# Neighbour sums of a graph network on one Trainium2 core: count strips in 4-byte form, source rows in two float32r parts instead of three bf16 parts

## What is computed

```python
def gin(x, src, dst, weights):                  # block 2
    for wa, ba, wb, bb in weights:              # 128->256->256, 256->256->256, 256->128->128
        h = x + segment_sum(x[src], dst)        # plain sums: every edge counts 1
        x = relu(relu(h @ wa + ba) @ wb + bb)
    return x
# block 4: h = segment_sum(norm_edge * (x @ W)[row], col), three times; norm from edge weights
x = layernorm(x + gat(x)); x = layernorm(x + gin(x))
x = layernorm(x + gat_edge(x)); x = layernorm(x + gcn(x, edge_weight))
```

## Time and profile before

| | us |
|---|---|
| time, median of 3 runs (lowest, highest) | 7460.89 (7459.09, 7463.34) |
| profiled execution, its own time | 7457.86 |
| its span from first to last instruction | 7456.0 |
| PE busy | 3668.1 |
| DVE busy | 3117.1 |
| POOL busy | 3331.8 |
| ACT busy | 955.4 |

### The profile page before, as it was taken

One profiled execution on the slowest core, in us unless ns is written; L12 is line 12 of the kernel. 1 busy time (PEld: TensorE's weight loads), 2 busy tenths in 40 slices (PEclk: granted clock), 3 DMA queues, 4 the chain that ended last, 5 costly groups with the idle time before them and its releaser, 6 DMA issues. The chain is left out here.

```text
span 7456.0 us, 44211 instructions
## 1 busy us (share of the span) xinstructions
PE 3668.1 (49%) x15287; PEld 1843.6 (25%) x15287; DVE 3117.1 (42%) x6406; ACT 955.4 (13%) x853; POOL 3331.8 (45%) x3338
## 2 busy tenths in 40 slices
PE   2000000000001999999999910000015999999997
PEld 1000000000000545544444410000013544544543
DVE  4566667699992122112225535555554000000002
ACT  1334341010000111000000003333310000000000
POOL 2777776677777553132226757777730000000000
PEclk7555555555555999999999955555557999999998
DMA  2565654059901554222246513334314888888886
GB/s 85 178 207 190 214 198 136 0 195 343 338 5 28 170 171 125 88 85 83 86 139 181 165 38 111 119 111 119 111 42 135 278 285 286 280 285 287 279 285 206
DMA packets 502264, 1242.48 MB, mean 167 GB/s; under 512 B 114034, under 2 KB 162648, under 8 KB 493080
## 3 DMA queue, kind: packets, MB, share of 16 engines
q1 hardware_dynamic: 382216, 1114.01, 44.4%
q0 software_dynamic: 119824, 125.65, 7.2%
HBM read 861.79 MB, written 377.50 MB: 166 GB/s over the span
## 5 line engine op out<-in xcount | busy, mean ns | idle before, releaser
L733 PE MATMUL psum<-gb,big 128*128 128x512 f16 (+2 forms) x7644 | 2383.8, 468 | 26.3 <-DVE turned L912 13.1
L571 POOL DMA_INDIRECT plane<-total,cell x1564 | 1644.9, 1052 | 1398.4 <-DVE gb L552 483.5
L336 POOL DMA_INDIRECT gb<-rows,src x1564 | 1486.9, 951 | 487.1 <-issue 475.7
L733 PEld LDWEIGHTS psum<-gb,big 128*128 128x128 bf16 (+1 forms) x7644 | 1040.6, 144 | 1189.4 <-issue 811.3
L733 PE MATMUL psum<-gb,x 128*128 128x512 f16 (+1 forms) x2548 | 621.9, 367 | 1212.5 <-DMA gb<-plane 1203.2
L1487 PE MATMUL psum<-identity,end_top 128*8 128x128 f32 (+1 forms) x2 | 0.7, 372 | 2123.4 <-DVE end_top L1564 2123.4
L733 PEld LDWEIGHTS psum<-gb,x 128*128 128x128 bf16 x2548 | 232.9, 98 | 1475.1 <-DMA gb<-plane 1204.3
L1472 ACT COPY gb<-turned 128x1632 f32<-128x1632 f32 (+3 forms) x138 | 450.8, 3267 | 721.9 <-DVE turned L1560 721.9
L912 DVE TENSOR_TENSOR turned<-psum,big 128x512 f32<-128x512 f32 (+1 forms) x39 | 25.5, 660 | 1214.5 <-PE psum L762 1214.5
L1487 PEld LDWEIGHTS psum<-identity,end_top 128*8 128x8 f32 (+1 forms) x2 | 0.2, 82 | 2123.8 <-DVE end_top L1564 2123.8
L529 DVE TENSOR_SCALAR_CACHE_REDUCE begun<-gb 128x1 f32<-128x1 f32 (+60 forms) x782 | 482.2, 617 | 59.2 <-PEq L1414 59.2
(11 more groups left out here) (298 smaller groups left out, 2940.5 us busy)
## 6 DMA issues: line engine op xcount, KB each, us to landing
gb<-plane SPq DMA_DIRECT2D x588, 512.0 KB, 4.5
gb<-plane SPq DMA_DIRECT2D x294, 576.0 KB, 4.8
plane<-turned SPq DMA_DIRECT2D x49, 3200.0 KB, 29.9
gb<-plane SPq DMA_DIRECT2D x588, 256.0 KB, 2.9
gb<-plane SPq DMA_DIRECT2D x294, 288.0 KB, 3.2
plane<-turned SPq DMA_DIRECT2D x49, 1600.0 KB, 11.0
runs<-gb SPq DMA_DIRECT2D x33, 1748.0 KB, 6.1
runs<-gb SPq DMA_DIRECT2D x33, 1610.0 KB, 5.7
```

What stands on the lines that cost most here:

```text
L336: m.s_rows[b % BUFS].up(nc.gpsimd.indirect_dma_start(m.batch(b, columns, row)[:, j, 0:width], None, table, bass.IndirectOffsetOnAxis(ap=m. ...
L571: done.up(m.nc.gpsimd.indirect_dma_start(plane, bass.IndirectOffsetOnAxis(ap=m.cell[:, r:r + 1], axis=0), total[:, r:r + 1], None), 16)
L733: mm = nc.tensor.matmul(m.psum[:, 3 * k + i, 0:nodes], rows, slot[:, a:a + nodes], start=begin, stop=False)
```

## The change

1. **Parts.** Source rows are kept as two parts of type float32r (4 bytes), a rounded high part and the rest. [...] In the wide layer the two parts of a source tile are made new in each step: the high one by ScalarE (`make_high`), the low one by VectorE (`make_low`). Landing slots for fp16 go from 7 to 5.
2. **Order.** A new function `count_layers` writes each engine's order by hand over all 882 steps. The nodes themselves are added inside the steps. Narrow layers use two sets of PSUM banks in turn. The weighing is spread evenly over the steps until 93% of the work instead of in shares before each result.
3. **Count.** One operation on all 782 columns, with a table of ones and 1024s in PSUM as second operand, gives count and "is last" together.
4. **Barriers.** The blocks are opened with `no_gpsimd_drain=True`.

```diff
-        for j in range(NARROW):
-            compare(m.total16[:, r:r + 1], 2 * r, r, 0, r + 1)
-            compare(m.following[:, b % 2, j:j + 1], 2 * r + 1, r, r, COLS)
+            m.s_compared.up(nc.vector.scalar_tensor_tensor(
+                m.unread[r % 2], m.key, m.key[:, r:r + 1], m.step[:, COLS - 1 - r:2 * COLS - 1 - r], ALU.is_equal, ALU.mult,
+                accum_out=m.total[:, r:r + 1]))
...
+    def lay(self, engine, n):
+        self.wait_landed(engine, n)
+        self.wait_used(engine, n - STRIPS)
+        out, landed = self.strip(n)[:, 0:self.width_of(n)], self.landing(n)[:, 0:self.width_of(n)]
+        if self.by_vector(n):
+            m.s_strip_dve.up(nc.vector.tensor_copy(out, landed))
+        else:
+            m.s_strip_act.up(nc.scalar.copy(out, landed))
+
+    def make_high(self, act, n):
+        self.wait_used(act, n - 2)
+        m.s_high.up(m.nc.scalar.activation(self.ring(n)[:, 0, :], self.source(s), ACT.Relu))
...
+        for k in range(self.blocks):
+            for part in range(PARTS):
+                if self.wide:
+                    rows = self.ring(n)[:, part, k * P:(k + 1) * P]
+                else:
+                    rows = (m.high, m.low_part)[part][:, s, :]
...
+                for _, i, tiles in quads_of(r):
+                    if s in tiles:
+                        mm = nc.tensor.matmul(m.psum[:, self.bank(r, k, i), c * P:(c + 1) * P], rows, m.identity_r[:, :], start=False, stop=False)
...
+                due = min(COLS, COLS * passed * 100 // (93 * sum(units)))
+                if not taken and due > weighed:
+                    weigh_edges(m, dve, weighed, due)
-    with m.nc.Block() as block:
+    with nc.Block(no_gpsimd_drain=True) as block:
```

More of the change, by code:

```diff
@@ new lines, in quad_of, with first_tiles, count_layers, net_before @@
+def quad_of(t):
+    return next(g for r in range(len(ROUNDS)) for g, _, tiles in quads_of(r) if t in tiles)
+def first_tiles():
+    return [tiles[0] for r in range(len(ROUNDS)) for _, _, tiles in quads_of(r)]
+def count_layers(*layers):
+    m = layers[0][0].m
+    nc = m.nc
+    steps = [(sums, take, *divmod(n, TILES)) for sums, take in layers for n in range(STEPS)]
+    units = [2 if sums.wide else 1 for sums, *_ in steps]
+    last = len(ROUNDS) - 1
+    def net_before(p):
+        if p == 0:
+            return None
+        sums, take, r, s = steps[p - 1]
+        before = sums.after if r == 0 else sums
+        if s % 5 != 4 or before is None:
+            return None
+        old = last if r == 0 else r - 1
+        if s // 5 >= len(quads_of(old)) * before.parts:
+            return None
+        return before, dict(layers)[before], old, s // 5
+    with nc.Block(no_gpsimd_drain=True) as block:
@@ L992, in _, with plane_layers @@
+        @block.tensor
+        def _(pe):
+            for sums, _ in layers:
+                sums.pe(pe)
+            layers[-1][0].last_net(pe)
+        @block.sync
+        def _(sp):
+            for sums, _ in layers:
+                sums.sp(sp)
+    m.settle()
+def plane_layers(*layers):
+    m = layers[0][0].m
+    with m.nc.Block(no_gpsimd_drain=True) as block:
+        @block.vector
+        def _(dve):
+            for sums, take in layers:
+                sums.dve(dve, **take)
         @block.scalar
@@ L1014, in plain_dense_stage @@
     dense = Dense(m, source, 1, [], weight, D, target)
-    with nc.Block() as block:
+    with nc.Block(no_gpsimd_drain=True) as block:
         @block.vector
@@ L1663, in selu_stage @@
     out, x, scratch = m.tmp[:, :, :], m.x[:, :, :], scratch_of(m)
-    rest, spare = m.half(0), out.rearrange("p t d -> p (t d)").bitcast(bf16)
-    first_parts = [spare[:, k * TILES * D:(k + 1) * TILES * D].rearrange("p (t d) -> p t d", d=D) for k in range(2)]
-    with nc.Block() as block:
+    rounded = m.half(0)
+    with nc.Block(no_gpsimd_drain=True) as block:
         @block.vector
```

391 lines of the change are left out of this document (268 added, 123 removed).

## The result

The changed kernel takes **6947.6 us** (median of 4 runs, 6945.1 to 6949.9) against 7460.0 (7458.2 to 7463.3) on the same chip: ratio 0.9314, 95% interval 0.9301 to 0.9327. The profiled execution has a span of 6946.3 us against 7456.0, so 509.7 us are to be found.

What follows compares the result with a forecast made beforehand. TensorE was taken to set the GIN stage's pace and GpSimd that of the stage ahead. The sum was 7456 - 27 - 508 + 33 + 38 - 52 = 6940 of span, with 1.9 around it 6942 us; range 6840 to 7110.

Steps and rivals of the forecast that it cites:

- term 2: GIN stage, 512-column products: 4704 left of 7056, each still at 0.216 us, so 508 us less.
- term 4: GIN stage, TensorE's new waits: strips 22, loading saved x 12, ring handshake 15, bank changes -11; sum +38 us.
- term 1: Start, the count stage ahead of the GIN stage: drain left out, faster count, one split gone; 27 us less.
- the stage: Sign: the GIN stage, 1925 us before, would take about 1435 us.
- TensorE's start: Sign: TensorE would start its products at about 2376 us.
- term 3: GIN stage, 128-column products: 1176 at 0.111 us in place of 1764 at 0.056, so +33 us.
- Term 5: End of the GIN stage: GpSimd no longer late, barrier at the last result, 4276 instead of 4328.16; 52 us less.
- The 4-byte operand at two cycles per column: Rival, GIN stage: float32r products stream as slowly as fp32 records; 7906 us, slower than before; chance 0.1.
- short products at 0.216: Rival, GIN stage: each 128-column product costs a full 0.216 us; +123, 7065 us; chance 0.15.
- Laying as the bound: Rival, GIN stage: casting strips from 2 to 4 bytes takes ScalarE 1.4 us; about +160, 7100 us; chance 0.08.
- The count on VectorE at 1.83 us a column: Rival, count stage: the slow PSUM operation makes it some 470 us longer; about 7420 us; chance 0.05.
- Short products at 0.056: Rival, GIN stage: 128-column products stay at 0.056 us and no new waits come; 6840 us; chance 0.12.

Runs made afterwards that it cites:

- experiment 1: The changed kernel with GpSimd's drain put back at the end of all its blocks: 6975.1 us, ratio 0.9352, +27 over the changed kernel.
- experiment 2: The kernel before with GpSimd's drain left out at the end of all its blocks: 7410.2 us, ratio 0.9932.
- experiment 3: The changed kernel with the old pair of comparisons per column in place of the one count operation, drains still out: 6967.9 us, ratio 0.9341.
- experiment 7: The changed kernel without the 392 identity products of 128 columns (own rows left out of the sums): 6912.5 us, ratio 0.9261.
- experiment 6: The changed kernel with 64 in place of 128 weight columns in 47 of each 49 tiles' GIN products: 6898.2 us, ratio 0.9243.
- experiment 9: Experiment 4's version with products reading strips where they land, 7 landing places and no copies: 6819.6 us, ratio 0.9139.
- experiment 8: Two runs of the changed kernel: all strips copied by ScalarE, 6950.9 us; only 64 columns copied after each layer's first four strips, 6947.2 us.
- experiment 4: The changed kernel with parts, strips, ring and identity as 2-byte fp16 in place of 4-byte float32r: 6835.2 us, ratio 0.9162.

## Why the prediction came out

The sum was 6942 and the time is 6947.6, but term 2 was off by 67 us one way, and term 4 by 43 and term 1 by 22 the other way. That they cancel to within 6 us is luck. Right were the engine that sets the stage's pace, TensorE, and the number of products that go. Of the signs that it named, the stage came at 1460.5 us where about 1435 was said, and TensorE's start at 2354 where 2376 was.

- **Term 1 (-27): -48.6.** The step that failed is "leaving the drain out gives back these 9.1 us", with the bounds 0 and 9.1. I took the barrier to fall at the end of GpSimd's last transfer at the latest. Without the drain it opens before that (1339.59 against 1353.50), and the drain is worth 27.0 and 26.4 us (experiments 1 and 2), of which 24.0 and 23.3 fall at this barrier. The count was taken at 1.01 us a column and is 0.95; its share is 16.4 (experiment 3) where the steps gave 9.6 (18.7 less 9.1). That GpSimd hides the rest of it was right.
- **Term 2 (-508) and term 3 (+33): together -475, measured -407.8**, as TensorE's busy time in the two windows. Term 2 is the mis-sized one: 0.227 us in a quiet stretch instead of 0.216 is 4704 x 0.011 = 52 us, and the mean of 0.230 over the stage makes it 4704 x 0.014 = 66 us, all of the difference. "Needs no such split" was right, since the product has one record and one pass; that it would therefore cost what a 2-byte one does was not. Term 3 holds: 0.115 us in the rows above and 0.096 by experiment 7, against 0.111. Its mechanism, the reload of 4-byte rows, is shown by experiment 6.
- **Term 4 (+38): -5.** TensorE has 15.4 us without a product instead of 20.4. Only 3.5 us of it are a wait for a strip. The 22 us of waiting for strips rested on a narrow step of 0.90 us against strips of 0.96. They would not have come even with products of 0.216: in experiment 9 a step has four of these and five steps with the network part between them take 5.21 us (3639.95 to 3645.16), 1.04 a strip, at a DMA share of 0.82. The mistake was to price the steps without network parts by themselves, where the strips that land during a network part are there for the steps behind it. The 15 us for the ring's handshake were never there (0.2). The waits for drained banks at the beginning of rounds, 10.0 and 4.4 us before (TensorE for L867 and L864), are gone, as the -11 had it.
- **Term 5 (-52): -52.2**, since GpSimd is done 73 us ahead ("some 80" was said of the weighing) and the barrier falls behind the last result. The number is right, the reason in part: 17.6 of the 52.2 us were not GpSimd being late but VectorE weighing its last 19 columns ahead of the last result, which the prediction took to be out at 4276. The even weighing until 93% moves both.
- **Rivals.** The 4-byte operand at two cycles per column, and short products at 0.216, did not happen (0.227 and about 0.11). Laying as the bound is refuted by experiment 8, where even all of it on ScalarE stays hidden, at 1.04 us a strip. The count on VectorE at 1.83 us a column did not happen. Short products at 0.056 is what the distance behind a short product suggests; experiments 4 and 6 show it to be the price of 2-byte or half-width rows only.

## What to carry to other kernels

A type that saves passes can still cost per product: here 11 ns on each beside a 2-byte one, and the weight load behind each short one. Count both before choosing two 4-byte parts where two 2-byte ones might carry enough digits. Price a short product by the whole repeating pattern, never by the distance to the next start, because a late load shows up one product further on. And a block's end is a wait like any other: leave the drain out where all that needs GpSimd's transfers waits for their semaphores itself (here `wait_cells`), and look for the gain where GpSimd is last. Before you put a stage's tail down to one engine, look for the last row of each: here two engines shared it.

## What the runs showed of the hardware

- A product of 4-byte operands at full clock takes its columns at 2.4 GHz and 13 ns more: 0.120 us for 256, 0.227 for 512 in a quiet stretch. Over the stage the long one takes 0.230, with 128 and with 64 weight columns. With 2-byte operands it is 0.216 for 512.
- Weight loads of 128 columns of 4 bytes follow each other every 0.11 us behind short products, and their records last 189 ns. Records of 128 columns of 2 bytes last 98 ns, of 64 columns of 4 bytes 135 ns.
- With GpSimd's drain the end of the block ahead of the count came 24 us later. Without it a block's end opened 14 and 31 us before GpSimd issued its last transfer.
- A two-input operation with a scalar, an accumulated result, PSUM as second input and as output takes VectorE 0.95 us for 782 columns, no more than from and to SBUF (0.96 for 765).
- 612 us less of ScalarE's copies beside the products (experiment 8) changed neither their distance nor the time.
